# Halves of the turned probabilities ahead of a slot's evictions, in the first 57 slots of a transformer layer

## The reference

```
x = x + layernorm(attention(layernorm(x)))
x = x + layernorm(ffn(layernorm(x)))

attention: q, k, v = x W_qkv, 16 heads of 32; q, k rotated (cos, sin);
           softmax(q k' / sqrt(32)) over keys with i - 128 <= j <= i, times v; then W_out + b_out
ffn:       up = x wu', gate = x wg'; (silu(up) * gate) wd', the three matrices rounded to
           -1, 0, 1 times mean|W| (2048 x 512 each)
```

## Time and profile before

| | |
|---|---|
| median of 3 runs | 1333.2 us |
| profiled execution | 1332.5 us |
| its span | 1330.3 us |
| PE busy | 1290.0 us (97%) |
| PE weight loads | 908.4 us (68%) |
| DVE busy | 941.2 us (71%) |
| ACT busy | 796.3 us (60%) |
| POOL busy | 708.4 us (53%) |
| share of PE in the chain that ended last | 82% |

### The profile page before, as it was taken

How to read it: one execution, slowest core, us unless ns; L and a number is a source line. 1 busy time by engine, 2 the same in 40 slices (tenths; PEclk the granted TensorE clock), 3 DMA queues, 4 the chain that set the end, 5 groups by cost and what they waited for, 6 DMA issues and landing times.

```text
span 1330.3 us, 28312 instructions
## 1 busy us (share of the span) xinstructions
PE 1290.0 (97%) x9948; PEld 908.4 (68%) x9948; DVE 941.2 (71%) x2421; ACT 796.3 (60%) x1468; POOL 708.4 (53%) x959
## 2 busy tenths in 40 slices
PE   8879988999999999999999999999999999999997
PEld 5566665767677676777677676776667777666775
DVE  6867978776778767886778767787778767634333
ACT  3788887556665665657566566656656566533332
POOL 3356796545555556555456456555465463425432
PEclk9999999999999999999999999999999999999999
DMA  6887967675587576876678666875758746610000
GB/s 231 288 278 235 270 186 150 152 130 131 126 173 171 110 161 139 161 152 125 139 150 170 136 124 135 178 162 114 152 119 170 135 99 122 126 36 25 25 17 32
DMA packets 397276, 190.75 MB, mean 143 GB/s; under 512 B 318800, under 2 KB 372432, under 8 KB 397136
## 3 DMA queue, kind: packets, MB, share of 16 engines
q1 hardware_dynamic: 396272, 187.37, 63.0%
q10 hardware_dynamic: 864, 1.57, 0.4%
HBM read 84.48 MB, written 25.17 MB: 82 GB/s over the span
## 4 chain that ended last, share of the span: by engine, by line
PE 82%; DVE 4%; POOL 4%; DMA 4%; ACT 3%; issue 3%; SPq 1%; POOLq 0%; ACTq 0%; DVEq 0%
PE J L1613 28%; PE Y L1630 16%; PE J L1550 12%; PE J L1560 7%; PE J L1541 7%; PE S L1613 5%; PE O L1525 4%; PE S L1493 2%; DMA spill<-split 1%; DVE prob L1272 1%; POOL swp L841 1%; DMA W<-in_w_qkv 1%; ACT prob L1025 1%; DVE turned L1282 1%; DMA parts<-in_w_up 0%
## 5 line engine op out<-in xcount | busy, mean ns | idle before, releaser
L1630 PE MATMUL Y<-down_q,room 128*128 128x512 fp8e4 x1024 | 262.3, 379 | 0.6 <-DVE room L1340 0.6
L1550 PE MATMUL J<-xnT,W 128*128 128x512 f32 x512 | 242.5, 600 | 0.7 <-ACT xnT L984 0.6
L1025 ACT ACTIVATE prob<-prob,peak 128x256 f32<-128x256 f32 x512 | 229.7, 498 | 10.8 <-DVE peak L1272 10.6
L1272 DVE CUSTOM_DVE_ANT_0 prob<-S,band,neg_score_scale 128x256 f32<-128x256 f32 x512 | 225.8, 478 | 12.0 <-PE S L1490 6.6
L1613 PE MATMUL J<-xT,gate_q 128*128 128x256 f16 x1760 | 210.2, 273 | 4.0 <-DVE room L1326 4.0
L1613 PE MATMUL J<-xT,up_q 128*128 128x256 f16 x1776 | 212.0, 273 | 1.9 <-DMA xT<-xs 1.9
L1078 ACT ACTIVATE room<-J,sig_scale 128x512 f32<-128x512 f32 x111 | 76.3, 687 | 218.8 <-PE J L1613 218.8
L1613 PEld LDWEIGHTS J<-xT,gate_q 128*128 128x128 fp8e4 x1760 | 171.4, 98 | 49.3 <-DVE room L1326 8.5
L1613 PEld LDWEIGHTS J<-xT,up_q 128*128 128x128 fp8e4 x1776 | 173.3, 98 | 45.8 <-issue 2.0
L1326 DVE SCALAR_TENSOR_TENSOR room<-room,J 128x512 f32<-128x512 f32 x111 | 76.4, 688 | 175.1 <-ACT room L1078 175.0
L875 POOL TENSOR_TENSOR o_n<-o_raw,rinv 128x128 f32<-128x128 f32 x128 | 53.8, 420 | 270.0 <-DVE rinv L1301 270.0
(11 more groups left out here) (159 smaller groups left out, 1976.5 us busy)
## 6 DMA issues: line engine op xcount, KB each, us to landing
spill<-split SPq DMA_DIRECT2D x64, 256.0 KB, 2.6
Qp<-spill SPq DMA_DIRECT2D x127, 128.0 KB, 2.9
Kp<-spill SPq DMA_DIRECT2D x125, 128.0 KB, 3.0
x_in<-in_x SPq DMA_DIRECT2D x32, 256.0 KB, 3.5
X<-in_x SPq DMA_DIRECT2D x32, 256.0 KB, 3.4
out_x<-X SPq DMA_DIRECT2D x32, 256.0 KB, 3.3
room<-in_w_gate SPq DMA_DIRECT2D x12, 512.0 KB, 7.0
room<-in_w_down SPq DMA_DIRECT2D x10, 512.0 KB, 4.9
```

What stands on the lines that cost most here:

```text
L1025: e = nc.scalar.activation(prob[:, prob_home(U), a, :], prob[:, prob_home(U), a, :], ACT.Exp, bias=peak[:, prob_home(U), a:a + 1], scale=-1.0)
L1272: e = nc.vector.tensor_tensor_reduce(out=prob[:, prob_home(U), a, :], in0=S_ps[U % 2][:, a * 2 * P:(a + 1) * 2 * P], in1=mask[:], scale=ne ...
L1550: e = pe.matmul(dst[:], W[:, part, c, g * P:(g + 1) * P], xnT[:, c, :], start=(c == 0), stop=(c == DC - 1))
L1630: e = pe.matmul(Y_ps[t][:], h[:, q % HELD, part, (a * HT + t) * P:(a * HT + t + 1) * P], down_q[:, 2 * pair + a, :], start=(pair == 0 and ...
```

## The change

In slots below `BY_PE` the loops of ScalarE and VectorE call `p_high` and `p_low` for the unit of that slot (unit s - 1) in front of the evictions of the jobs that end there, not behind them. Slot 58 and those after it keep their order. TensorE, GpSimd and SyncE keep theirs throughout. ScalarE's queue changes in 13 slots, VectorE's in 28.

```
--- before.py
+++ after.py
@@ -1141,10 +1141,14 @@
                 i, u = divmod(s, UNITS)
                 if s + 1 < ALL_UNITS:
                     exp(s + 1)
+                if s < BY_PE:
+                    for U in high_units(s):
+                        p_high(U)
                 for job in ENDS[s]:
                     empty(job)
-                for U in high_units(s):
-                    p_high(U)
+                if s >= BY_PE:
+                    for U in high_units(s):
+                        p_high(U)
                 for job in ENDS[s - 2] if s >= 2 else ():
                     if job[0] in ("Q", "K"):
                         rotated_high(job)
@@ -1429,10 +1433,14 @@
                 i, u = divmod(s, UNITS)
                 if s + 2 < ALL_UNITS:
                     logits(s + 2)
+                if s < BY_PE:
+                    for U in high_units(s):
+                        p_low(U)
                 for job in ENDS[s]:
                     empty(job)
-                for U in high_units(s):
-                    p_low(U)
+                if s >= BY_PE:
+                    for U in high_units(s):
+                        p_low(U)
                 for job in planes_at(s, MERGE_X, MERGE_O):
                     if job[0] == "OT" or job[1] % 2 == 0:
                         merge_words(job)
```

## The result

| | before | changed |
|---|---|---|
| median | 1333.99 us (20 runs, 1332.29 to 1337.46) | 1337.29 us (20 runs, 1334.55 to 1340.99) |
| profiled execution | 1332.5 us | 1338.48 us |
| its span | 1330.3 us | 1336.3 us |
| PE busy | 1290.0 us (97%) | 1292.1 us (97%) |

The ratio is 1.0018 with a 95% interval of 1.0010 to 1.0026: the changed kernel is slower by about 2.4 us (1.3 to 3.5). (The two medians of the table are 3.3 us apart, 0.25%, which lies inside that interval; in what follows the loss is taken by the ratio, as 2.4.) The prediction was 1333.7 us, in a range up to 1336.0; the time lies 3.6 us above the one and 1.3 above the other. As a ratio the loss is just under the 0.2% that the prediction called measurable, and with 20 runs a side it is measured.

The account below looks back on a forecast made before the run. From 216.1 us TensorE is the bound, so the first feed-forward matmul's start decides; before it no single engine is. Terms 0.2 + 0 + 0.3 - 0.5 - 0.1 + 0 + 0.6 = +0.5 us gave 1333.7 us, range 1331.0 to 1336.0.

Parts of the forecast that it names:

- slot 54: Q of tile 2: low ahead of the shuffle delays GpSimd, spill and the feed-forward's turned input; +0.6 us, bounds 0.3 and +0.7.
- the 1110.9 us behind the first feed-forward matmul: Stretch after the first feed-forward matmul, held fixed; a change by over 1 us would show the prediction wrong.
- Slot 2: Q of group 2: shuffle 1.28 us later, its spill perhaps absorbed by the DMA backlog; +0.2 us, bounds 0 and +1.2.
- Up to 102.24: Slot 22's scores wait 1.20 us for group 3's packing, absorbing everything TensorE gains or loses before; 0.
- Slots 22 and 23: Q and K of tile 1: K's shuffle, spill and pack late, scores at 123.80 start later; +0.3 us, bounds 0 and +0.6.
- Slot 31: V of tile 1: high runs in ScalarE's idle time, TensorE's 0.48 us wait goes; -0.5 us, bounds -0.6 and 0.
- Slots 33 and 35: VectorE saturated: logits follow a shuffle, saving 0.21 us each, but low may wait for high; -0.1 us, bounds -0.6 and +0.3.
- the rule weighed in the prediction: Skill's VectorE rule: a semaphore between two operations costs nothing extra; by it the slots 33 and 35 term would be +0.3.
- Slots 36 to 52: GpSimd's queue hides late shuffles; xnT matmuls at 195.17 start 0.5 us later, taken up behind; 0, bounds 0 and +0.5.
- A: Transposes' waits for lows behind evictions come back, 4.6 us in five waits; 1328.6 us, chance 0.10.
- B: Rotation chain not covered: late shuffles of slots 2, 22, 23, 54 and late xnT reach 216.11; 3.0 us, 1336.2, chance 0.12.
- C: Nothing arrives: transfers and GpSimd's queue hold everything, including slot 54; 1333.2 us, chance 0.25.

Follow-up runs that it names:

- e1: Changed kernel with the halves moved ahead only in the Q and K slots; ratio to the kernel before 1.0019 (1.0008 to 1.0030).
- e4: Changed kernel with the halves moved ahead only in slots 24 to 57; ratio to the kernel before 1.0013 (1.0003 to 1.0023).
- f2: Kernel before with the halves moved ahead in slots 54 and 55 alone; ratio to the kernel before 1.0015 (1.0001 to 1.0029).
- g2: Kernel before, with SyncE issuing the turn of the feed-forward's input ahead of slot 56's other transfers; ratio to the kernel before 0.9990 (0.9980 to 1.0001).
- g4: Halves moved in all slots but 54 and 55, turn issued ahead of slot 56's other transfers; ratio to the kernel before 0.9985 (0.9974 to 0.9997).
- e3: Changed kernel with the halves moved ahead only in slots 1 to 23; ratio to the kernel before 1.0009 (1.0000 to 1.0017).
- g1: Changed kernel plus nine identity products in front of TensorE's wait for the feed-forward's input; ratio to the kernel before 0.9992 (0.9982 to 1.0001).
- g3: Changed kernel, with SyncE issuing the turn of the feed-forward's input ahead of slot 56's other transfers; ratio to the kernel before 0.9993 (0.9983 to 1.0002).
- f3: Changed kernel plus 16 identity products in front of TensorE's wait for the feed-forward's input; ratio to the kernel before 1.0008 (0.9993 to 1.0023).
- e2: Changed kernel with the halves moved ahead only in slots without a Q or K job; ratio to the kernel before 1.0010 (0.9998 to 1.0022).
- f1: Changed kernel with the halves moved in all slots but 54 and 55; ratio to the kernel before 0.9990 (0.9977 to 1.0003).
- f4: Kernel before plus 14 identity products ahead of the feed-forward and 12 ahead of slot 22's scores; ratio to the kernel before 1.0007 (0.9993 to 1.0021).

## Why the prediction was wrong

**The step that failed is slot 54, "+0.6; bounds 0.3 and +0.7", with the sentence that what comes before 216.1 "is passed to the end unchanged" and the stretch behind it held fixed.** The mechanism was the right one, link by link: low half first, shuffle +0.6, GpSimd +0.6, spill and turn +0.76, first product +0.79, and the moved low half of slot 55 fits into the wait for the sum (0.95 us became 0.59) and costs nothing there. Its size was not: the term measured 0.8 in the chain and 1.4 in this execution (1.6 in e1, 1.7 in e4 and f2) of clock behind it, 2.2 to 2.4 together. (Of the 0.8, 0.6 are the low half; another 0.16 come in between GpSimd's product and the spill, and why was not looked into.) The prediction took a wait on TensorE as worth its length. Its own list of what would show it wrong had "a change of the 1110.9 us behind the first feed-forward matmul by over 1 us"; from the first product to the end of the span it is now 1336.3 - 220.56 = 1115.7 us, and before it was 1330.3 - 216.11 = 1114.2, so 1.5 more, of which 1.4 are over by the first gate product. (The 1110.9 was itself a wrong difference of the rows, which give 1114.2.)

The trace of the kernel before had shown such a drop already, 26 us ahead of the feed-forward, in rows that the prediction did not weigh. TensorE waits 1.94 us for an attention sum, and from 1.1 us behind that wait its granted clock is 0.50 for 3.4 us:

```profile
190.14 0.19 PE L1525 MATMUL O<-Vc,turned 128*128 128x66 f16 x1 [1.94 <-DVE o_raw L1296]
...
192.00:194.00 2.00, 1.88 (x15) 1.69 (x14) 1.35 (x4) 2.00 (x5) 1.68 (x6) 0.50 0.93 288
```

A wait of 1.88 us that is about to grow by 0.6 was to be weighed against this one.

The Trainium skill ("TensorE: Matmul & The Clock Gate", HAM oscillation — how this bites in real kernels) describes a kernel whose TensorE waits some 3 to 5 us for data between groups of products, and whose next group starts cold each time. The rows here agree that products behind a wait can start at the lower clock, 3.31 us against 1.91 for the same 16; but the waits that did it here are shorter, 2.54 us in this trace, and the measured ones decide.

**Which waits drop the clock here.** At the feed-forward 2.54, 3.27, 3.29 and 3.30 us were followed by 1.2 GHz, and 1.84 (twice), 1.87 and 1.88 were not. In front of the scores of slot 22 it was dropped after 2.02, 2.07, 2.09, 2.67, 2.69, 3.01 and 3.28 us and kept after 0.56, 1.08, 1.20, 1.42 and 2.12. So near 2 us either may happen, and the kernel before stood at 1.88: the later chain made this one wait longer than any here that kept the clock. What else enters (the phase, the work just before) was not tried.

**Slot 2, forecast +0.2.** Shuffle +1.28 as forecast; the pack did not move, in this trace or in the others with the new order. The lower bound, 0, was the truth.

**Up to 102.24, forecast 0.** Nothing speaks against it: where there is a wait, TensorE's gains end in it. But this wait is itself a large source of scatter. It is 1.20, 2.12 and 3.01 us in three executions whose order is the old one up to there (before, f2, g2; also 2.02 in e4), and 3.28, 2.09, 2.07, 1.42, 1.08 and 0.56 in six with the new one (g4, changed, e3, g1, g3, f3); e1 and e2, each with a part of the early changes, have 2.67 and 2.69, and f1 has none. Its length does not follow the order. When it is long the clock drops behind it, and the packing of slot 22's Q comes 1.1 to 1.7 us later against its logits (issue of the spill 12.0 to 12.3 us behind them, 10.6 to 10.9 where the clock was kept; g4 13.1 and f1 11.3 stand apart).

**Slots 22 and 23, forecast +0.3.** Changed (g1, g3, f3) and unchanged (before, f2, f4) executions without the drop have 10.93 to 10.94 and 10.60 to 10.66 us from the logits to the spill. That is the 0.3. (The working in the prediction gave two numbers, 0.35 for Q's sum and 108.28 - 108.07 = 0.21 for K, and called both 0.3.) The wait of the scores of slot 30 (near 123.8 before) was to grow by it. In the changed trace it is 0.95 us with the clock's drop mixed in; in the six without the drop it is 0.21, 0.51 and 1.03 with the old order (before, f4, f2) and 1.36, 1.72 and 1.76 with the new one (g1, f3, g3), and these scores come 21.1 to 21.9 us behind the logits of slot 22 with the old order and 21.7 to 22.1 with the new. The sign is right; the scatter of 0.8 us within one order is too wide to put the size at 0.3.

**Slot 31, forecast -0.5.** Measured 0.48, with the wait of 0.48 gone. It stands in other traces too: from the scores of slot 30 to the transposes of slot 37 it is 19.15 us in five with the new order (e2, e4, f3, g1, g3) and 19.63 to 19.64 in five with the old (before, e3, f2, f4, g2). It doesn't all stay: up to the transposes of slot 39 it is 26.1 to 26.5 us with the new order (changed, e4, f3, g1, g3, g4; f1, whose clock drops in slot 30, has 27.8) and 26.3 to 27.3 with the old (before, e3, f2, f4, g2), 26.45 against 26.51 in the pair of the forecast.

**Slots 33 and 35, forecast -0.1.** Logits follow the shuffle by 0.64 us and not the low half by 0.82; the low half waits 0.24 us for its high at 139.26. Both signs are as forecast, and they cancel: from the transposes of slot 34 to those of slot 37 it is 8.24 us in either order. On the rule weighed in the prediction this trace has nothing new: in the changed order no logits stand right behind their own low half in these slots.

**Slots 36 to 52, forecast 0, with +0.5 from the xnT copies taken up behind.** The wait in slot 53 grew from 0.98 us (five of six executions with the old order; 0.35 in that of before, where the clock had dropped four us earlier) to 2.12 (seven of eight with the new one). From the transposes of slot 52 to those of slot 54 it is 7.68 us in the old order (e1, e3, f2, f4) and 8.28 to 8.29 in the new (e4, g1, g4), 0.6 more, each without a drop of the clock there; from the same start to the logits of slot 54 it is 10.47 and 10.22 to 10.26: given back and 0.2 more. Where the clock drops behind that wait (changed, e2, f3, g3) it is 10.73 to 10.88. So the term is -0.2 or +0.4 by the clock, near 0 as forecast.

**Rivals.** A, 1328.6: the waits for low halves did fall, by 2.8 us where it counted 4.6, and the kernel got slower; the waits for the attention sums, which it left out, stayed at 12.1 us. B, 1336.2: nearest in time and wrong in its place; it wanted a pack of group 2 over 0.8 us late, and that pack did not move. The prediction's C, that nothing arrives (not the theory C of the experiments): refuted by the first feed-forward product, 0.79 us later behind slot 54's logits, and by f2. What no rival named was a price on the far side of the point that was taken as the end of the change.

**What stays open.** e2 and e3, which leave slots 54 and 55 alone, are 1.3 and 1.2 us slower, f1, which contains both, 1.3 us faster; the intervals of e2 and f1 reach past 0, and that of e3 touches it. So these runs don't tell the sign of what the rest of the change is worth; f1, whose interval ends at +0.4, tells that it is not the 2.4. And g1 gained 1.7 us more than its one execution explains. Its mean clock is higher than the changed kernel's by 0.0022, nearly two stretches and not one, so it seems to have kept the clock more often at some other place as well; that this makes up the 1.7 us is not shown.

## What to carry to other kernels

A wait on TensorE can have two prices: its length, and the products behind it at half the clock. Here the second came behind every wait of 2.46 us or more that was looked at, and behind some of those near 2 us; so ask of a sub-microsecond delay not only whether it arrives, but how long the wait already is at which it arrives, and look in the trace for the granted clock behind other waits of that length. When a chain ends in an engine's wait, look at what stands ahead of the awaited transfer in the issuing queue: taking the turn out from behind a spill brought the first feed-forward product 2.1 us nearer in the trace, and g2 measured -1.3 us (-2.7 to 0.1). And when cheap filler products are tried, measure how long they take first; nine did it, sixteen cost more than the wait.

## What the hardware showed beyond what was expected

- The stretch at 1.2 GHz behind the first feed-forward product lasts 3.4 us and costs 1.4 to 1.7 us there, where TensorE is the bound (changed, e1, e4, f2); one of the same length behind the xnT products of slot 53, where other waits follow, costs 0.5 to 0.6 us by the logits of slot 54 (changed, e2, f3, g3).
- Waits of 0.56 to 1.88 us in front of slot 22 and of the feed-forward never dropped the clock, those of 2.46 us or more from 102 us to the feed-forward, at these two places and at the attention products near 184 us, always did (ten of ten). Of the 25 waits between 1.91 and 2.13 us in the same stretch of the 14 traces, 15 did. One drop stands at the end of a wait of 0.99 us (slot 53 of g2), with waits of 1.92 and 0.98 us in the 5 us ahead of it.
- A 128x128 float32 product of the identity shows as two matmuls: 9 take 2.25 us and 16 take 3.81, about 0.24 each.
- The same kernel's executions differ by up to 9.5 us (1331.39 to 1340.86 in one set of 35). The profiled ones differ above all ahead of the scores of slot 30: the transposes of slot 22 start between 99.7 and 104.3 us, and from there to those scores it is 23.4 to 28.0 us. With 11 or 12 runs against 35 the intervals here are 1.1 to 1.9 us to either side; one trace against one trace showed 6 us for a difference of 2.4.
